# A decoder layer on one core: four edits to TensorE's order, in the self attention's scores, the cross attention's probabilities, the feed-forward and the last image

## What is computed

```python
x = _layernorm(x + attn(x))          # 16 heads of 16, causal, softmax over 256 keys
x = _layernorm(x + xattn(x, ctx))    # 16 heads of 64, 77 keys of a context, softmax
x = _layernorm(x + ffn(x))           # 512 -> 1024 -> 1024 -> 256, weights +1 or -1, relu
```

## Time and profile before

| what | us |
|---|---|
| median of 3 runs | 2189.83 |
| lowest, highest run | 2187.28, 2194.01 |
| the profiled execution, its own time | 2191.86 |
| its span, first to last instruction | 2190.1 |
| mean granted TensorE clock | 0.99 |

### The profile page before, as it was taken

How to read it: one execution, slowest core, us unless ns; L and a number is a source line. 1 busy time by engine, 2 the same in 40 slices (tenths; PEclk the granted TensorE clock), 3 DMA queues, 4 the chain that set the end, 5 groups by cost and what they waited for, 6 DMA issues and landing times.

```text
span 2190.1 us, 54589 instructions
## 1 busy us (share of the span) xinstructions
PE 2112.3 (96%) x18572; PEld 1868.8 (85%) x18572; DVE 1501.4 (69%) x4647; ACT 1134.8 (52%) x2571; POOL 669.8 (31%) x751
## 2 busy tenths in 40 slices
PE   8998689999999999999999999999999999999998
PEld 7887578888888888888888888888888888888887
DVE  5553467777777777777777777777777777777764
ACT  5554445555555545555555555445555555555553
POOL 2000223333333333233333333333333333333331
PEclk9999899999999999999999999999999999999999
DMA  8997532233333333322333333333223332333310
GB/s 270 310 295 208 133 72 63 63 72 73 56 65 77 77 77 77 72 66 62 70 73 63 58 77 77 77 77 75 65 63 67 73 67 54 77 77 77 77 44 10
DMA packets 180580, 196.57 MB, mean 90 GB/s; under 512 B 50131, under 2 KB 135155, under 8 KB 180467
## 3 DMA queue, kind: packets, MB, share of 16 engines
q1 hardware_dynamic: 180532, 195.94, 38.6%
HBM read 69.37 MB, written 58.87 MB: 59 GB/s over the span
## 4 chain that ended last, share of the span: by engine, by line
PE 82%; ACT 6%; issue 4%; DVE 4%; DMA 2%; SPq 1%; POOL 1%; ACTq 0%; POOLq 0%; DVEq 0%
PE ps L1202 13%; PE ps L1385 11%; PE ps L1243 9%; PE ps L1244 9%; PE ps L1351 5%; PE ps L1279 5%; PE ps L1211 4%; PE ps L1226 3%; PE ps L1294 3%; PE ps L1268 3%; PE ps L1369 3%; PE ps L1183 2%; ACT probs L651 2%; PE ps L1152 2%; PE ps L1254 2%
## 5 line engine op out<-in xcount | busy, mean ns | idle before, releaser
L1243 PE MATMUL ps<-r_h,w 128*128 128x256 f16 x2048 | 461.9, 273 | 1.6 <-DVE r_l L843 1.6
L1244 PE MATMUL ps<-r_l,w 128*128 128x256 f16 x2048 | 460.6, 273 | 0.0
L857 DVE CUSTOM_DVE_ANT_0 junk<-ps,causal 128x128 bf16<-128x128 f32 (+1 forms) x1024 | 331.2, 356 | 127.1 <-PE ps L1268 116.2
L503 POOL TENSOR_SCALAR_AFFINE_SELECT probs<-probs 128x512 f32<-128x512 f32 x256 | 163.3, 638 | 465.0 <-ACT probs L651 460.7
L526 POOL TENSOR_TENSOR rstd<-var_eps,minus_half 128x2 f32<-128x2 f32 x96 | 66.9, 696 | 670.5 <-DVE var_eps L832 670.5
L626 ACT ACTIVATE p2r<-ps,low 128x77 f32<-128x77 f32 x1024 | 243.2, 340 | 43.6 <-DVE low L896 42.9
L517 POOL TENSOR_TENSOR p<-p2r,inv 128x308 f32<-128x308 f32 x256 | 201.2, 787 | 196.6 <-DVE inv L907 192.8
L1385 PE MATMUL ps<-vo_h,p2t 128*128 128x256 f32 (+1 forms) x1280 | 239.4, 290 | 8.0 <-DVE p2t L914 8.0
L1243 PEld LDWEIGHTS ps<-r_h,w 128*128 128x128 f16 x2048 | 200.2, 98 | 35.7 <-issue 9.5
L589 ACT ACTIVATE r_h<-ps 128x512 f16<-128x512 f32 x256 | 148.8, 597 | 154.0 <-PE ps L1244 139.2
L843 DVE SCALAR_TENSOR_TENSOR r_l<-ps,r_h 128x512 f16<-128x512 f32 x256 | 172.9, 686 | 75.3 <-ACT r_h L589 75.2
(11 more groups left out here) (145 smaller groups left out, 4736.2 us busy)
## 6 DMA issues: line engine op xcount, KB each, us to landing
vo_scratch<-vo_out SPq DMA_DIRECT2D x80, 448.0 KB, 5.3
vo<-vo_scratch SPq DMA_DIRECT2D x64, 512.0 KB
q_st<-p2t SPq DMA_DIRECT2D x192, 128.0 KB
k_bd<-p2t SPq DMA_DIRECT2D x192, 128.0 KB, 6.4
q<-q SPq DMA_DIRECT2D x128, 128.0 KB, 2.1
k_bd<-k_scratch SPq DMA_DIRECT2D x64, 154.0 KB, 3.5
x_in<-in_x SPq DMA_DIRECT2D x32, 256.0 KB, 2.7
out<-y SPq DMA_DIRECT2D x32, 256.0 KB, 6.4
```

The source lines that it names most:

```text
L857: dve.tensor_tensor_reduce(out=junk[:, e, b * P:b * P + width], in0=ps[:, bank + b, e * width:(e + 1) * width], in1=causal[:, (1 - b) * P: ...
L1243: pe.matmul(dst, w1[:, kk, m * P:(m + 1) * P], r0_h[:, kk, :], start=kk == 0, stop=False)
L1244: last = pe.matmul(dst, w1[:, kk, m * P:(m + 1) * P], r0_l[:, kk, :], start=False, stop=kk == KF - 1)
```

## The change

It moves calls in PE's list and reorders one tuple, in four places:

1. `scores_by_key(i, 4)` goes from behind `values(i, 1)` to ahead of `queries_keys(i + 1, 0)`, and `layer0(f, 1)` from behind `scores_by_key(i, 6)` to ahead of it.
2. The unit with the partial tile becomes the first of a group: `P2T_UNITS` is ((4,), (0, 1), (2, 3)), and the flags that start and end the sum in PSUM follow it.
3. In the cross attention, parts 20 to 22 of `layer1` are laid elsewhere, and the transposes of unit 2 of each group go ahead of the output of unit 0.
4. In the tail, the first parts of `layer1` each wait for the relu that they read, not for three. The calls of `layer2` there are written out, in the same order as before.

```diff
-        P2T_UNITS = ((0, 1), (2, 3), (4,))
+        P2T_UNITS = ((4,), (0, 1), (2, 3))
...
-            def layer1(f, q):
+            def layer1(f, q, last_banks=False):
...
-                    pe.wait_ge(d_r0, nth(f, 4, max(q + 1, 3)))
+                    pe.wait_ge(d_r0, nth(f, 4, q + 1 if last_banks else max(q + 1, 3)))
...
-                                             start=g == 0 and n == 0 and k == 0 and b == 0,
-                                             stop=g == 1 and n == VT - 1 and k == 2 and b == TB - 1)
+                                             start=g == 0 and n == P2T_UNITS[0][0] and k == 0 and b == 0,
+                                             stop=g == 1 and n == P2T_UNITS[2][1] and k == 2 and b == TB - 1)
...
+                scores_by_key(i, 4)
                 if more:
                     queries_keys(i + 1, 0)
                 values(i, 0)
                 values(i, 1)
-                scores_by_key(i, 4)
                 scores_by_key(i, 5)
                 filler0(0)
+                filler0(1)
                 scores_by_key(i, 6)
-                filler0(1)
...
-                layer1_until(f, 19, 20)
+                layer1_until(f, 19, 21)
                 cross_scores(i, 7, f)
                 cross_transposes(i, 0, 0)
                 cross_transposes(i, 0, 1)
-                layer1_until(f, 20, 22)
+                layer1_until(f, 21, 22)
+                cross_transposes(i, 0, 2)
                 cross_output(i, 0, 0)
-                cross_transposes(i, 0, 2)
+                layer1_until(f, 22, 23)
                 cross_output(i, 0, 1)
                 cross_output(i, 0, 2)
                 cross_transposes(i, 1, 0)
                 cross_transposes(i, 1, 1)
                 next_scores(3)
-                layer1_until(f, 22, 24)
+                layer1_until(f, 23, 24)
+                cross_transposes(i, 1, 2)
                 cross_output(i, 1, 0)
-                cross_transposes(i, 1, 2)
                 cross_output(i, 1, 1)
                 next_scores(4)
                 cross_output(i, 1, 2)
...
-            layer1_until(B - 1, 0, 4 * KF)
-            for blocks in (range(0, 6), range(6, KF)):
-                for b in range(TB):
-                    layer2(B - 1, b, blocks, 6)
+            for q in range(4 * KF):
+                layer1(B - 1, q, last_banks=True)
+            layer2(B - 1, 0, range(0, 6), 6)
+            layer2(B - 1, 1, range(0, 6), 6)
+            layer2(B - 1, 0, range(6, KF), 6)
+            layer2(B - 1, 1, range(6, KF), 6)
```

## The result

The changed kernel takes 2222.44 us (median of 4 runs, 2222.30 to 2222.78), the kernel before in the same comparison 2190.89 us. The ratio is 1.0143, with a 95% interval of 1.0130 to 1.0156. The profiled execution took 2222.36 us, its span is 2220.6 us, the mean granted clock 0.99.

A forecast was written before the change was run, and what follows sets the result against it. PE's order of work was taken to bound the kernel (82% of the chain). Turns 1 to 30 at +0.78 us (+23.4) plus the ends gave +28.2 us, 2218 us against the runs; range 2201 to 2238.

The forecast's parts named there:

- The landing: Self attention: the maxima's DMA lands at 1208.9 in image 16, so scores by key 4 wait 1.4 us.
- Part 1: Self attention, scores by key 4 ahead of queries and keys: +0.86 us a turn, bounds +0.7 to +1.2.
- Parts 2 and 3: Cross attention: 0.61 us of waits gone, 0.53 new, -0.08 us a turn, bounds -0.6 and +0.4.
- Image 0: First image: queries, keys and values come behind the DMA, partly at half clock: +4 us, bounds 3 to 6.
- Image 31: Last image: values no longer cover the DMA wait, part given back at scores 6: +1.5 us.
- The tail: Layer 1 after the loop: its first two parts can start sooner, giving back 0.7 us, bounds 0 and 1.1.
- A: DVE behind the late self output: slack used up, up to 0.7 us a turn more, 2239 us; chance 0.12.
- B: PE in every turn: some 10 us at half pace, +5 us x 30, 2370 us; chance 0.04.
- C: Ahead of scores 4: short DMA wait, nil from 1207.5 on; faster, 2160 to 2172 us; chance 0.07.
- D: Whole kernel: all parts reach their lower bounds, +8 us or a little less, within 0.3%; chance 0.07.

The follow-up runs named there:

- The run with one issue: Changed kernel with the maxima of heads 8 to 15 copied by one DMA in place of two: 2201.20 us, ratio 1.0035.
- the one with three: Changed kernel with one more small DMA (4 x 128 bytes to a spare tile) issued ahead of the two: 2252.39 us, ratio 1.0266.
- the kernel before with an extra issue: Kernel before with one more small DMA (4 x 128 bytes to a spare tile) ahead of the two: 2190.58 us, ratio 0.9997.
- the run of it alone: Kernel before with only the cross attention's changes (units' order, layer 1 parts, unit 2's transposes first): 2186.77 us, ratio 0.9984.

## Why the prediction was right, and where its terms were off

The time was forecast as 2218 us and came out as 2222. The mechanism was right: one wait for the maxima's DMA ahead of scores 4, at the size and place said, in every turn of the loop. That the sum came so close is in part luck, since errors of 4 us and of 2 us in it went opposite ways. Step by step:

**The landing.** I took it from image 31, where the kernel before shows the wait without large loads ahead of it, as 3.30 us behind the maxima or 2.48 behind the issue. In the loop of the changed kernel scores 4 came 3.49 and 2.59 us behind. In its own image 31 the number is 3.30 again:

```profile
2136.90 0.38 PE L1329 MATMUL ps<-ident,row_max 128*8 128x128 f32 x2
...
2140.20 0.74 PE L1279 MATMUL ps<-q_st,k_bd 128*128 128x256 f32 x4 [1.62 <-DMA q_st<-neg_max]
```

So the loop's DMA lands 0.1 to 0.2 us later than the last image's. Why isn't known. An obvious suspect is the loads of value outputs: in the 0.5 us behind the issue the DMA share is 0.95 in image 16 and 0.34 in image 31. But in image 1 of the same trace all DMA engines are busy in those 0.5 us (303.42 to 303.92), and scores 4 still come 3.29 us behind the maxima, so the loads alone don't explain it. No run took them away. The run with one issue and the one with three confirm the mechanism in both directions, and the kernel before with an extra issue shows the cover.

**Part 1, +0.86 us a turn.** The maxima to layer 0 part 0 took 6.39 us before and 7.57 now (1221.18 to 1228.75), less what scores 4 and part 1 give back. The whole turn is 0.91 longer; with 0.05 for the cross attention in the run of it alone, part 1 costs 0.96. The term was 0.10 too small, which is what the landing came later than said (3.49 in place of 1208.9 - 1205.51 = 3.39). That scores 6 would find ACT ready held: in the rows above they start at 1229.65 without a bracket.

**Parts 2 and 3, -0.08.** Alone they gave -0.05 a turn. The new waits that I laid out are there, with other sizes: 0.19 for unit 2's transposes (0.32 said), 0.11 for the output of unit 1 (0.07 said) and 0.22 for the last output (0.14 said). Their sum is 0.52 where I had 0.53, so these errors cancelled. The waits of 0.25 and 0.36 that the change aimed at are gone. A step that removes 0.6 us of waits gained a tenth of that. The likely reason, which no run isolates, is that the chain through ACT and DVE that set them is about as long as before and only the place where PE meets it moved.

**Ends.** Image 0: I said +4, bounds 3 to 6. The maxima of images 0 and 1 are now transposed at 233.89 and 302.61, before at 234.26 and 300.89, so that turn is 2.1 us longer, below my bounds. Queries and keys and values do come behind the DMA there, but less of the turn ran at half clock (columns as above; the kernel before, then the changed one in two stretches):

```profile
242.40:249.00 6.60, 6.55 (x32) 6.12 (x36) 2.18 (x2) 3.09 (x5) 2.14 (x3) 0.52 0.05 18
...
242.10:245.30 3.20, 3.20 (x15) 3.20 (x16) 0.00 (x0) 0.00 (x0) 0.00 (x0) 0.50 0.00 0
...
245.30:252.00 6.70, 5.92 (x75) 4.45 (x74) 2.75 (x4) 4.91 (x9) 1.91 (x3) 0.99 0.13 42
```

Behind its wait the kernel before was at half clock for some 6.6 us, the changed one for 3.2. Half of the difference, 1.7 us by estimate, is what the term lacks. Nothing in the change aims at that. Image 31 cost more than I said: from its maxima to the end of the span it takes 83.7 us in place of 82.5, and with the 0.7 us that the tail gave back that is 1.9, forecast was 1.5. The tail: DVE's four low parts start at 2195.64 and the span ends 24.96 us later, before it was 25.67 (2164.43 to 2190.1), 0.7 us as forecast. In the trace:

```profile
2196.38 0.28 PE L1243 MATMUL ps<-r_h,w 128*128 128x256 f16 x1
...
2196.98 0.28 PE L1243 MATMUL ps<-r_h,w 128*128 128x256 f16 x1
...
2197.58 0.28 PE L1243 MATMUL ps<-r_h,w 128*128 128x256 f16 x1
```

Each part starts 0.6 us behind the former, at DVE's pace, not three at once.

**Sum.** Between the profiled executions the change costs 30.5 us (2191.86 to 2222.36), forecast were 28.2: the turn was 30 x 0.13 = 4 us too small, image 0 about 2 us too large, and the other ends make up the rest within 0.5 us. Against the medians it is 31.6 us, since the profiled execution of the kernel before lies 1 us above the median of its four runs.

**Rivals.** A (the late start runs through to DVE): not seen, no wait for relus or keys came up. B (the clock): not in the changed kernel, whose clock stayed full from image 2 to the end, but it was closer than I gave it credit for, as the extra issue shows; when it fell there, it cost 1.6 us in 4 turns and 2.8 in a fifth, not 5 us in every turn. C (the DMA lands early enough): it landed at a time that answers to 1209.0, 1.5 us behind the 1207.5 that C needed. D: no.

## What to carry to other kernels

A wait travels with the call that has it: before moving a call ahead, look up when each thing that it waits for arrives, and not only the gap that it is to fill. If that wait never shows because other work covers it, look for a turn that lacks the cover (a first or last iteration); it can show the latency that the loop hides. And a gap that is filled by shuffling work along the same chain can come back at the next meeting point (0.61 us of waits gone, 0.52 new here), so check which wait is next in that chain before counting the gain.

## What the hardware showed that I had not expected

Whether PE's clock falls behind a wait isn't told by the length of that wait alone. Idling of 1.36 us in each turn of 61 us never lowered it in the loop. Idling of 2.00 us did in 5 of 29 turns of one kernel, at 1.6 us each in most, and not in the other 24. In image 1 of the changed kernel the clock was at 0.64 from 306 to 309 us, behind waits of 0.67, 1.02 and 2.04 us within 6 us, while a single wait of 2.25 us in image 31 of the kernel with one issue more left it at 1.00.

And a third tiny DMA issue (512 bytes) holds up the reader of the two behind it by 0.64 us. For these small copies on SP it is the issue that counts, not the bytes, since one DMA of 8 KB did the work of two of 4 KB in 0.74 us less.
